# Loads of turn 1 from ScalarE's queue, two residual chunks loaded later, and unused matrix products ahead of the logits, in a row and column attention kernel on one core

## What is computed

```python
Qs = (q0 @ Wq_s) * scale_s                      # q0: row 0 of the normalised x
sw = softmax(Qs @ (x @ Wk_s)^T over the rows)   # a weight per row, column and head
Q = (x @ Wq) * scaling * sw
K, V = x @ Wk, x @ Wv
QK = einsum('brihd,brjhd->bhij', Q, K)          # logits: 192 x 192 per head, summed over rows
attn = softmax(QK)
out = x_in + einsum('bhij,brjhd->brihd', attn, V)
```

## Time and profile before

| | |
|---|---|
| median of 3 runs | 540.41 us (537.84 to 541.54) |
| the profiled execution | 543.76 us, its span 542.0 us |
| TensorE busy | 93% of the span |
| VectorE, ScalarE, GpSimd busy | 72%, 51%, 35% |
| mean granted TensorE clock | 0.982 of full |
| DMA moved | 134.44 MB, mean 248 GB/s |

### The profile page before, as it was taken

One profiled execution on the slowest core, in us unless ns is written; L12 is line 12 of the kernel. 1 busy time (PEld: TensorE's weight loads), 2 busy tenths in 40 slices (PEclk: granted clock), 3 DMA queues, 4 the chain that ended last, 5 costly groups with the idle time before them and its releaser, 6 DMA issues.

```text
span 542.0 us, 16054 instructions
## 1 busy us (share of the span) xinstructions
PE 503.0 (93%) x6346; PEld 393.7 (73%) x6346; DVE 392.2 (72%) x1056; ACT 275.5 (51%) x574; POOL 190.6 (35%) x236
## 2 busy tenths in 40 slices
PE   7669997999999999999899999995999979999995
PEld 5558754555555555555699988895999979998884
DVE  2879988888888888887566686652676744677763
ACT  4568577779999999974222110031655631211000
POOL 3003347658877777772200000022566540000000
PEclk9999999999999999999899999997999979999999
DMA  8999022664777766998989999999979566987997
GB/s 328 377 418 378 2 114 92 206 214 140 231 233 234 235 221 209 225 226 151 243 207 292 312 337 315 350 287 342 283 264 331 196 167 199 323 274 264 252 244 207
DMA packets 186271, 134.44 MB, mean 248 GB/s; under 512 B 168992, under 2 KB 170848, under 8 KB 186208
## 3 DMA queue, kind: packets, MB, share of 16 engines
q1 hardware_dynamic: 153664, 120.88, 71.2%
q10 hardware_dynamic: 32544, 12.68, 9.6%
HBM read 76.92 MB, written 56.62 MB: 246 GB/s over the span
## 4 chain that ended last, share of the span: by engine, by line
PE 78%; DVE 8%; DMA 6%; ACT 3%; POOL 2%; issue 1%; SPq 0%; DVEq 0%; POOLq 0%; ACTq 0%
PE PS L1217 25%; PE PS L1225 13%; PE PS L1312 11%; PE PS L1316 6%; DMA EXTRA<-in_x 5%; DVE EXTRA L773 5%; PE PS L1347 3%; PE PS L1348 3%; PE PS L1351 3%; PE PS L1349 3%; PE PS L1350 3%; POOL EXTRA L505 1%; DMA EXTRA<-xt_scratch 1%; PE PS L1178 1%; PE PS L1190 1%
## 5 line engine op out<-in xcount | busy, mean ns | idle before, releaser
L1217 PE MATMUL PS<-WP,EXTRA 128*128 128x384 f16 (+1 forms) x1152 | 160.0, 289 | 6.5 <-DMA EXTRA<-xt_scratch 5.8
L1217 PEld LDWEIGHTS PS<-WP,EXTRA 128*128 128x128 f16 x1152 | 98.5, 99 | 50.5 <-issue 24.5
L505 POOL TENSOR_TENSOR EXTRA<-BIG,EXTRA 128x512 f16<-128x512 f32 x69 | 83.6, 1213 | 31.9 <-ACT EXTRA L604 24.2
L545 POOL TENSOR_TENSOR BIG<-EXTRA,BIG 128x384 f32 x48 | 43.8, 914 | 134.9 <-ACT BIG L715 131.7
L1225 PE MATMUL PS<-WP,EXTRA 64*128 64x384 f16 (+1 forms) x1152 | 83.6, 286 | 0.0
L1225 PEld LDWEIGHTS PS<-WP,EXTRA 64*128 64x128 f16 x1152 | 48.0, 95 | 29.4 <-issue 17.3
L511 POOL TENSOR_TENSOR BIG<-EXTRA,BIG 128x192 f16<-128x192 f32 x96 | 53.8, 560 | 35.7 <-ACT BIG L658 35.7
L722 ACT CAST BIG<-PS 128x384 f32 (+1 forms) x48 | 23.0, 480 | 78.4 <-PE PS L1225 69.2
L1312 PE MATMUL PS<-BIG,EXTRA 128*128 128x128 f16 x960 | 62.1, 219 | 0.3
L1312 PEld LDWEIGHTS PS<-BIG,EXTRA 128*128 128x128 f16 x960 | 53.8, 98 | 4.8 <-issue 0.5
L773 DVE BATCH_NORM_STATS2 EXTRA<-BIG 128x6 f32<-128x512 f32 x72 | 43.9, 679 | 14.5 <-ACT BIG L559 14.5
(11 more groups left out here) (189 smaller groups left out, 930.3 us busy)
## 6 DMA issues: line engine op xcount, KB each, us to landing
EXTRA<-in_x SPq DMA_DIRECT2D x24, 768.0 KB, 10.2
xt_scratch<-EXTRA SPq DMA_DIRECT2D x24, 768.0 KB, 3.7
BIG<-v_scratch SPq DMA_DIRECT2D x48, 384.0 KB, 5.2
EXTRA<-xt_scratch SPq DMA_DIRECT2D x24, 768.0 KB, 5.9
v_scratch<-EXTRA SPq DMA_DIRECT2D x32, 384.0 KB, 3.9
EXTRA<-in_x SPq DMA_DIRECT2D x24, 384.0 KB, 5.0
BIG<-in_x SPq DMA_DIRECT2D x24, 384.0 KB, 6.5
out_x<-BIG ACTq DMA_DIRECT2D x18, 384.0 KB, 6.0
```

The lines of the kernel that those rows point to most:

```text
L505: pool.tensor_tensor(tt[:, t, 1, :].rearrange("p (q n) -> p q n", n=P), raw(c, t), tt[:, t, 0, :].rearrange("p (q n) -> p q n", n=P), ALU. ...
L1217: ins = mm(outs[a], xt[:, t, s, q * P:(q + 1) * P], WP[:, t, w, wc], start=first and j == 0, stop=last and j == 2, skip_group_check=True)
```

## The change

The change does three things. The four loads of turn 1 are taken from SyncE and issued by ScalarE in `body(0)`, each behind the copies that follow the second of the two groups which used the same buffer. On SyncE the loop over turns now begins with turn 2; residual chunk 6 stands behind turn 3's loads and chunk 7 behind turn 4's. And TensorE gets `keep_awake` ahead of both logits: 18 products into bank 7 once all row weights are made, and 26 products into bank 6 once the keys' low parts of 45 of the 48 groups of the second projection are done.

```diff
+        def load_xt(eng, c, b):
+            eng.dma_start(XT[b], xt_dram[bass.ds(c, 1), :, :].rearrange("a p n -> p (a n)")).then_inc(s_xt[b], 16)
...
-                    for first, last, n in ((1, 2, 6), (2, 4, 7), (4, TURNS, 0)):
+                    for first, last, n in ((2, 4, 6), (4, 5, 7), (5, TURNS, 0)):
                         with sp.Fori(first, last) as t:
                             for b in range(4):
                                 sp.wait_ge(s_pj[1], (4 * t + b - 3) * 2)
-                                load_xt(4 * t + b, b)
+                                load_xt(sp, 4 * t + b, b)
                         if n:
                             sp.wait_ge(s_out[n], 48)
                             load_x(1, n)
...
                         if g or not isinstance(t, int):
                             q_high1(n - 1, g - 1)
+                        if isinstance(t, int) and g % 2:
+                            load_xt(act, 4 + g // 2, g // 2)
...
-            def keep_awake(n):
+            def keep_awake(n, bank=0):
                 for _ in range(n):
-                    mm(PS[:, 0, 0:256], two[:, 0:P], two, start=True, stop=True)
+                    mm(PS[:, bank, 0:256], two[:, 0:P], two, start=True, stop=True)
...
+                if h:
+                    pe.wait_ge(s_kvl[1], NG1 - 3)
+                    keep_awake(26, 6)
+                else:
+                    pe.wait_ge(s_sw, NCH)
+                    keep_awake(18, 7)
                 pe.wait_ge(s_ql[h], (NG1 if h else NG0))
                 pe.wait_ge(s_kvl[h], (NG1 if h else NG0))
```

More of the change, by code:

```diff
@@ L419, in _ @@
                 store_v(c)
-            def load_xt(c, b):
-                sp.dma_start(XT[b], xt_dram[bass.ds(c, 1), :, :].rearrange("a p n -> p (a n)")
-                             ).then_inc(s_xt[b], 16)
             for k in range(2):
@@ L466, in _ @@
                     for b in range(4):
-                        load_xt(b, b)
+                        load_xt(sp, b, b)
                 for n in range(HALF - 1, NRC):
```

## The result

| | before | changed |
|---|---|---|
| median of the runs | 540.97 us (4 runs, 537.84 to 543.74) | 533.8 us (4 runs, 532.9 to 537.03) |
| ratio to before, 95% | | 0.989 (0.9846 to 0.9934) |
| profiled execution, its time | 543.76 us | 532.90 us |
| its span | 542.0 us | 531.2 us |
| granted clock over the span | 0.982 | 0.990 |

The account below looks back on a forecast made before the run. TensorE was taken to bound the kernel, losing time to waits (chiefly turn 1's late load) and half-clock work after them. 5.05 + 2.7 + 3.05 - 0.2 = 10.6 us; 540.4 - 10.6 = 529.8 us, range 526.5 to 536 (8 in 10).

Parts of the forecast that it names:

- signs of being wrong: First load over 4 us behind ScalarE's last store, ScalarE's copies slipping over 1 us, or a new turn-boundary wait over 1 us.
- The load comes sooner: Start of turn 1, second projection: first load lands at 369.1, so the turn begins then, not at 374.15; 5.05 us won.
- The 2.1 us behind the last store: Turn 1's first load on ScalarE lands 2.1 us behind ScalarE's last output store, from a range of 1.8 to 2.5.
- The first logits' 1.7 us swallowed at turn 1: Full clock at the first logits brings TensorE 1.7 us earlier, but it only waits longer for turn 1's load; not added.
- the wait vanished: Rival at turn 1: stores end 1.7 us earlier, load lands as TensorE comes, 1.7 us more won; 528.1 us, chance 0.13.
- Turn 1's half-speed stretch, 2.7 us: Behind turn 1's wait: the remaining 1.85 us wait keeps the clock, so the half-clock stretch from 374.2 goes; 2.7 us won.
- The loads land no sooner: Rival at turn 1: saturated shared DMA engines land the loads at 373.9 as before; 537.4 us, chance 0.12.
- Chunk 6 at nothing: Residual chunk 6 moved before turn 4's loads: 0.2 us there, as chunk 7 cost before; turn 2's loads go sooner, unpriced.
- Chunk 7, 0.2 us: Residual chunk 7 moved one turn on, before turn 5's loads: 0.2 us lost there.
- Second logits, 3.05 us: Before the second logits: 26 unused products fill 2.8 of 3.19 us idle, so the logits run at full speed; 3.05 us won.
- The carry-over: The 10.6 us from the profiled execution (543.76 us) taken whole off the 540.4 us median, giving 529.8 us.

Follow-up runs that it names:

- changed again: The changed kernel once more, without an edit, with more executions: 534.17 us of 6 runs, ratio 0.9855 to the kernel before.
- only the products: The kernel before with both batches of unused products (18 and 26) and nothing else: 538.47 us, ratio 0.9961.
- only loads and chunks: The changed kernel without either batch of unused products: 538.76 us, ratio 0.9896 to the kernel before.
- without the first batch: The changed kernel without the 18 products ahead of the first logits, with the 26: 534.41 us, ratio 0.9894 to the kernel before.
- chunks last: The changed kernel with residual chunks 6 and 7 moved behind turn 5's loads on SyncE: 533.5 us, ratio 0.9879 to the kernel before.
- loads on SyncE: The changed kernel with turn 1's loads back on SyncE behind its nine stores; products and late chunks stay: 540.38 us, ratio 0.9997 to the kernel before.
- chunk 6 early: The changed kernel with chunk 6 right behind SyncE's stores, ahead of turn 2's loads, and chunk 7 ahead of turn 4's: 537.85 us, ratio 0.997.
- three stores fewer: The changed kernel with both chunks behind turn 5's loads and the first half's output chunk 4 stored by SyncE, not ScalarE: 534.31 us, ratio 0.9897.
- shorter second batch: The changed kernel with both chunks behind turn 5's loads, no first batch, and 9 products in place of 26: 535.37 us, ratio 0.9927.
- one store moved: The changed kernel with both chunks behind turn 5's loads and the last third of output chunk 4 stored by SyncE: 532.46 us, ratio 0.9829.
- one store moved, no products: The kernel of one store moved, without either batch of unused products: 534.87 us, ratio 0.9884 to the kernel before.

## Why the prediction was right, and where it was not

The direction, the mechanism and the range held: 533.8 lies within 526.5 to 536. The point of 529.8 was 4.0 us too low. One of its own signs of being wrong came out: a new wait over 1 us at a turn boundary, 1.34 us at turn 5.

**The load comes sooner: right, but mis-sized, 5.05 us against 6.7.** Turn 1 began at 367.44, not 369.1; in the second profile of the changed kernel at 368.97, close to the forecast. The mis-sized part is when ScalarE's stores end. Counted from the end of TensorE's first projection (us; "last v" is the last load of v in the first half landed, "asks" is when TensorE wants turn 1's first load):

| kernel | last v | ScalarE's last store landed | load issued, landed | TensorE asks | wait |
|---|---|---|---|---|---|
| before | 69.9 | 106.4 | 106.9, 113.0 (SyncE) | 107.5 | 5.76 |
| changed | 67.0 | 103.2 | 97.2, 105.8 | 106.0 | 0 |
| changed again | 68.4 | 105.8 | 98.6, 107.8 | 106.7 | 1.25 |
| only the products | 67.6 | 104.3 | 104.7, 110.8 (SyncE) | 106.0 | 5.04 |
| only loads and chunks | 69.5 | 106.5 | 99.0, 108.5 | 107.5 | 1.19 |
| without the first batch | 65.1 | 101.3 | 98.9, 105.4 | 107.2 | 0 |
| chunks last | 67.6 | 104.9 | 97.5, 106.9 | 106.5 | 0.61 |
| loads on SyncE | 67.2 | 103.6 | 104.6, 110.6 (SyncE) | 105.7 | 5.11 |
| chunk 6 early | 67.1 | 105.1 | 97.2, 107.0 | 105.7 | 1.53 |
| three stores fewer | 67.4 | 95.1 | 97.2, 103.4 | 105.6 | 0 |
| shorter second batch | 66.2 | 102.8 | 99.5, 106.4 | 107.9 | 0 |
| one store moved | 66.4 | 99.8 | 97.2, 104.3 | 105.6 | 0 |
| one store moved, no products | 66.8 | 100.1 | 99.0, 104.6 | 107.4 | 0 |

With its 15 stores ScalarE's last one lands 36.2 to 38.0 us behind the last load of v, in every row that has them. That load lands at 65.1 to 69.9 from one execution to the next, with the first batch or without. The prediction took 106.1 for the store from one execution that was the latest of these but for one; the others with 15 stores have 101.3 to 105.8. Why the loads of v vary so stays open.

**The 2.1 us behind the last store: right.** 2.6 us in the changed profile, 1.9 to 2.0 in the four others in which TensorE waits. Where the stores end sooner the load takes 5.6 to 7.1 us from its issue; in the two such rows with 15 stores that is 4.1 and 3.6 us behind the last store. In the changed profile the load was issued at 358.62, 1.8 us before the 360.4 of the prediction: 0.5 us because it goes out when the copy of queries ahead of it begins and not when it ends, the rest because that copy came 1.3 us sooner.

**The first logits' 1.7 us swallowed at turn 1: right in one execution and wrong in the other.** In the changed profile the stage is 1.64 us shorter, turn 0 comes sooner by as much and takes 0.48 us more than the 12.31 us of an undisturbed turn (0.6 of waiting was said; for what, the rows don't tell), and no wait at turn 1 takes the gain back. So the wait vanished, as one rival had it, but not for its reason: the stores ended sooner without following TensorE's clock. Most of the gain went at turn 5 instead, as the run without the first batch shows. In the second profile 1.25 us of waiting at turn 1 takes most of it. The times don't tell: 534.41 us without the batch against 533.8 and 534.17 with it.

**Turn 1's half-speed stretch, 2.7 us: right** at 2.58. Waits of 0.61 to 1.53 us at turn 1 kept the clock, as was assumed of 1.85; the waits of 5.04 and 5.11 us lost it. That 1.85 us would have kept it is not shown: it was taken from a wait of 1.97 us, and in four other executions one of 1.96 us at that place lost the clock (last section).

**The loads land no sooner: refuted.** The load landed 6.7 us sooner, and loads back on SyncE gives 540.38 us, at a ratio of 0.9997. The engines are shared all the same: SyncE's last store landed 115.1 to 119.0 us behind the end of the first projection in the seven profiles with the loads on ScalarE and nine stores on SyncE, against 108.8 to 111.2 in the three with the loads on SyncE. The loads go ahead at the expense of SyncE's stores, for whose landing TensorE does not wait. The rule of the Trainium skill named there, DMA: Bandwidth & Descriptors, "Issuing engines are not separate DMA queues", holds in what it says of sharing. It calls the issue time that is saved usually small beside the transfer; here it was not: the load was issued 9.1 us sooner (358.62 against 367.73), against 6.19 us from issue to landing in the earlier trace rows.

**Chunk 6 at nothing: right as a sum, incomplete as an argument.** Where it now stands it costs nothing in the changed profile and 0.3 us in the second (turn 3 takes 12.65 us), but left early it cost 5.06 us and a half-speed stretch at turn 2. The prediction said that turn 2's loads "now go when turn 1's parts are done" and put no price on what would happen otherwise.

**Chunk 7, 0.2 us: mis-sized.** It was 1.34 us in the changed profile, 0.45 in the second and 0.88, 0.29 and 0.51 in those of only loads and chunks, without the first batch and loads on SyncE. It held SyncE for 6.31 us and not the 5.24 of the earlier trace rows. With the chunks last the wait is gone.

**Second logits, 3.05 us: right** at 2.86, with a wait of 0.36 us.

**The carry-over is what failed.** The terms as they came in this pair of profiles are 5.44 + 1.64 + 0.17 + 2.58 + 0.19 + 2.86 - 1.50 - 0.54 - 0.01 = 10.83 us, as large as the 10.6 forecast. That they agree so well is partly luck: the 1.64 us that the sum left out makes up for the 1.50 lost at turn 5. The second profile of the changed kernel is 9.4 us under that of before. The medians differ by 7.2, because the profiled execution of before was 2.8 us above its median (543.76 against 540.97) and that of after 0.9 us below (532.90 against 533.8): 7.2 + 2.8 + 0.9 = 10.9. The prediction saw the distance, said that no row explains it, and carried the whole sum over.

The runs explain much of it: half-speed stretches differ from one execution to the next. In 62 executions of the kernel before on three chips (one of 1214.92 us is left out) the granted clock was 0.970 to 0.993 and the time 535.25 to 546.49 us. The 37 under 0.984 have a median of 542.97 us, the 25 others 539.04. The traces show what differs. Behind the 5 us wait at turn 1, turn 1 took 14.89 us in the profile of before, but 13.97 and 14.11 with only the products and with the loads on SyncE, against 12.31 undisturbed: a loss of 1.7 to 2.6 us. The second logits took 47.10 us there and 46.92, 45.88 and 45.88 in the three other profiles where they lost the clock, against 44.24: a loss of 1.6 to 2.9 us. So the 2.7 and 3.05 us of the sum come from the largest stretches of their kind. That these two stretches are ever missing where the wait is left, no trace shows; all profiles with the wait have them. Early stretches do come and go: the changed profile has two, from 25.2 and 93.4 us, and the second profile of the same program none, and in the three profiles with stretches from 40 to 41 and from 95 to 96 us the first projection ends at 263.3 to 263.6 us, against 260.1 to 261.2 in the five without any. How much of the 2.8 us each adds stays open. The median of the 62 is 542.3 us, so the three runs shown were on the low side too; against that the changed kernel's second median, 534.17, is 8.2 us less.

## What to carry to other kernels

A load that TensorE will want stands best in a queue whose stores drain before it is wanted, and what stands behind it on the old queue has to be moved with it, or the stall goes to the next load. Before a gain read from one profile is taken off a median, sort its terms: a wait for work that is always there can be carried over whole, a half-speed stretch only at the size that several executions show; the granted clocks of the timed runs tell whether the profiled one is like them. Unused products help when they leave little of the wait: 26, which left 0.36 us of it, kept the clock, and 9, which left 2.21 us, did not.

## What the runs showed of the hardware that was not expected

Which wait costs the clock isn't told by its length alone. At the logits, waits of 2.21 to 2.25 us were followed by half clock in every profile that had them. In the kernel before a wait of 2.29 us to 25.43 kept it. In the changed kernel at the same place a shorter one lost it, and in the second execution of the same program one as short kept it (TensorE's timeline and the window of the first, then of the second):

```profile
24.90 1.33 PE L1115 MATMUL PS<-ident,EXTRA 128*128 128x128 f32 x6 [1.88 <-DMA EXTRA<-in_x]
...
25.20:28.50 3.30, 3.13 (x16) 2.73 (x15) 1.01 (x2) 0.95 (x1) 0.00 (x0) 0.50 1.07 358
...
25.15 1.53 PE L1115 MATMUL PS<-ident,EXTRA 128*128 128x128 f32 x12 [1.86 <-DMA EXTRA<-in_x]
...
25.20:28.50 3.30, 2.06 (x17) 1.83 (x18) 1.59 (x4) 1.44 (x1) 0.00 (x0) 1.00 1.07 357
```

After 1.88 us of waiting the next 3.3 us ran at 0.50; after 1.86 us they ran at 1.00. A wait of 1.95 to 1.97 us to about 39.5 us, the same in twelve of the 13 profiles, was followed by half clock in four of them and not in eight. No part of the change touches these places; what decides it stays open.

A queue's backlog holds the engine that issues: one chunk of three loads held SyncE for 3.78 and 6.31 us in the changed kernel, where a load of turn 0 took 0.33 to 0.58 us to issue. And the issue of a DMA on ScalarE does not wait for the end of the copy ahead of it: turn 1's first load and that copy both begin at 358.62 us, and within 0.01 us of one another in all ten profiles with the loads on ScalarE.
